# Three more output products from rounded parts, and the sums of the third right operand one step earlier

## What is computed

```python
Q = (img_embed @ Wq).reshape(B, -1, H, D).transpose(0, 2, 1, 3)
K = (sent_embed @ Wk).reshape(B, -1, H, D).transpose(0, 2, 1, 3)
V = (sent_embed @ Wv).reshape(B, -1, H, D).transpose(0, 2, 1, 3)
score = jnp.einsum('bhqd,bhkd->bhqk', Q, K) / math.sqrt(D)
attn = jax.nn.softmax(score, axis=-1)
ctx = jnp.einsum('bhqk,bhkd->bqhd', attn, V).reshape(B, -1, H * D)
out = ctx @ Wo + img_embed
return (out - mu) * jax.lax.rsqrt(var + EPS) * gamma + beta
```

## Time and profile before

| | us |
|---|---|
| median of 3 runs | 355.93 (355.36 to 355.99) |
| the profiled execution | 354.91 |
| its span, first to last instruction | 353.1 |
| granted TensorE clock, mean | 0.999 of full speed |
| PE, PEld busy | 347.5, 323.9 |
| DVE, ACT, POOL busy | 265.1, 228.6, 193.0 |

### The profile page before, as it was taken

How to read it: one execution, slowest core, us unless ns; L and a number is a source line. 1 busy time by engine, 2 the same in 40 slices (tenths; PEclk the granted TensorE clock), 3 DMA queues, 4 the chain that set the end, 5 groups by cost and what they waited for, 6 DMA issues and landing times. The chain is left out here.

```text
span 353.1 us, 6783 instructions
## 1 busy us (share of the span) xinstructions
PE 347.5 (98%) x2272; PEld 323.9 (92%) x2272; DVE 265.1 (75%) x495; ACT 228.6 (65%) x778; POOL 193.0 (55%) x208
## 2 busy tenths in 40 slices
PE   9999999999999999999999999999999999999994
PEld 6999999999999999998899899988988998899884
DVE  2159998673921277898798988987988989879896
ACT  3267764244333569887876976878768769778560
POOL 0045640000003857679679688687696796885243
PEclk9999999999999999999999999999999999999999
DMA  8999779775735070052242341541522413403003
GB/s 236 425 420 337 255 240 338 274 250 211 228 137 202 0 278 22 3 179 97 84 151 70 137 152 38 172 137 43 180 90 91 149 65 144 148 32 120 32 35 114
DMA packets 19682, 55.80 MB, mean 158 GB/s; under 512 B 1728, under 2 KB 3264, under 8 KB 17728
## 3 DMA queue, kind: packets, MB, share of 16 engines
q1 hardware_dynamic: 18784, 54.38, 42.8%
q10 hardware_dynamic: 864, 1.00, 1.1%
HBM read 46.98 MB, written 8.39 MB: 157 GB/s over the span
## 5 line engine op out<-in xcount | busy, mean ns | idle before, releaser
L646 PE MATMUL pair<-vw_hi,pt_hi 128*128 128x512 f32 x155 | 62.2, 402 | 0.0
L646 PE MATMUL pair<-vw_hi,pt_lo 128*128 128x512 f32 x155 | 60.9, 393 | 0.0
L646 PE MATMUL pair<-vw_lo,pt_hi 128*128 128x512 f32 x155 | 60.5, 391 | 0.0
L1250 POOL TENSOR_TENSOR out_sb<-centred,beta_sb 128x512 f32<-128x512 f32 x30 | 38.8, 1294 | 28.9 <-ACT centred L840 28.8
L1270 POOL TENSOR_TENSOR x_sum<-xt_in 128x256 f32<-128x256 f32 x16 | 11.9, 745 | 62.2 <-DMA xt_in<-x_tiles 62.1
L795 ACT ACTIVATE prob<-c,neg_max 128x77 f32<-128x77 f32 x128 | 44.0, 346 | 0.0
L1295 POOL TENSOR_TENSOR xo_lo<-x_sum,xo_hi 128x512 fp32r<-128x512 f32 x32 | 41.6, 1304 | 0.5 <-ACT xo_hi L819 0.5
L571 PE MATMUL pair<-a_hi,xo_hi 128*128 128x308 f32 x128 | 40.4, 316 | 0.0
L571 PE MATMUL pair<-a_hi,xo_lo 128*128 128x308 f32 x128 | 38.9, 304 | 0.0
L571 PE MATMUL pair<-a_lo,xo_hi 128*128 128x308 f32 x128 | 38.9, 304 | 0.0
L833 ACT ACTIVATE pt_hi<-pair 128x640 fp32r<-128x640 f32 x32 | 22.5, 703 | 23.5 <-PE pair L633 23.5
(11 more groups left out here) (119 smaller groups left out, 945.0 us busy)
## 6 DMA issues: line engine op xcount, KB each, us to landing
w_out<-wo SPq DMA_DIRECT2D x8, 1024.0 KB, 4.8
xt_in<-x_tiles SPq DMA_DIRECT2D x16, 512.0 KB, 3.8
x_in<-x_rows SPq DMA_DIRECT2D x16, 512.0 KB, 4.8
out<-out_sb SPq DMA_DIRECT2D x31, 256.0 KB, 2.2
w_out<-wq_t SPq DMA_DIRECT2D x7, 1024.0 KB, 7.8
w_proj<-wv SPq DMA_DIRECT2D x8, 768.0 KB, 4.7
w_proj<-wk SPq DMA_DIRECT2D x6, 768.0 KB, 9.6
w_out<-wq_t SPq DMA_DIRECT2D x2, 512.0 KB, 7.9
```

The lines of the kernel that those rows point to most:

```text
L646: mm = pe.matmul(ps_out[:, i % 2, 0:s.model], ps[:, j, :], v[:, b, j, :], start=(j == 0 and n == 0), stop=(j == s.key_t - 1 and n == len(p ...
L1250: pool.tensor_tensor(out_sb[i % OUT_RING][:, :], centred[i % 2][:, :], beta_sb[:, :], ALU.add)\
```

## The change

The output products of steps 12, 13 and 14 (`SPLIT_VALUES`, value heads 4 to 6) take the form of rounded parts. For each of these: V is rounded and split into `kv_t`; Wo is rounded by ScalarE one step ahead, behind `split_vw`, and split by VectorE; ScalarE copies the first column range into `vw_t`, and VectorE adds the second in a new step `add_out_product`, with a semaphore `dve_vw_sum` on which later transposes and products wait. A gap in memory puts `v_t1` under `kv_t1`.

Since the rests and the rounded weights use the scratch of the sums, T3 comes earlier: at step 10 VectorE splits T2 and sums T3 ahead of `split_vw`, and ScalarE rounds T3 at step 10, in the same place as T4, ahead of VW's half 0; it was at step 11. T4 and T3 are split on VectorE behind `split_vw` at step 10.

```diff
+    SPLIT_VALUES = range(H + 4, USES - 1)
...
         def whole_out(u):
 
-            return u < FULL_OUT or u >= H
+            return u < FULL_OUT or (u >= H and u not in SPLIT_VALUES)
...
             def wait_out(u, half):
 
                 if u < H:
                     pe.wait_ge(dve_a_lo, 2 * u + half + 1)
+                elif whole_out(u):
+                    pe.wait_ge(act_vw_t, 2 * (u - H) + half + 1)
                 else:
-                    pe.wait_ge(act_vw_t, 2 * (u - H) + half + 1)
+                    pe.wait_ge(dve_vw_sum, summed_before(u) + half + 1)
...
             def transpose_vw(h):
                 for j, b in plan[h]:
                     n, rows = group_no[j, b], s.key_rows(j)
                     pe.wait_ge(act_vw_t, 2 * h)
+                    pe.wait_ge(dve_vw_sum, summed_before(H + h))
...
                 if u == H + 1:
                     for part in T_PARTS[:4]:
                         round_t(*part)
-                elif u in (H + 2, H + 3):
-                    for part in T_PARTS[2 * (u - H):2 * (u - H) + 2]:
+                elif u == H + 2:
+                    for part in T_PARTS[4:]:
                         round_t(*part)
...
                     split_vw(u - H)
-                if FULL_OUT <= u + 1 < H:
+                if u + 1 < USES and not whole_out(u + 1):
                     round_w_out(u + 1)
                 take_out_product(u, 1)
...
+            def add_out_product(u, half):
+
+                cols = head_cols(vw_t, half, u - H)
+                dve.wait_ge(act_vw_t, 2 * (u - H) + half + 1)
+                dve.tensor_tensor(cols, by_batch(second(ps_outp[half])), cols, ALU.add).then_inc(dve_vw_sum, 1)
...
+                if u == H + 2:
+                    for n, task in ((T2, split_t), (T3, right_sum)):
                         for b in range(s.batches):
-                            right_sum(n, b)
-                elif u in (H + 1, H + 2):
-                    for n in ((T1, T4), (T2, T3))[u - H - 1]:
-                        for b in range(s.batches):
-                            split_t(n, b) if n in (T1, T2) else right_sum(n, b)
-                elif u == H + 3:
-                    for n in (T4, T3):
-                        for b in range(s.batches):
-                            split_t(n, b)
+                            task(n, b)
+                if not whole_out(u):
+                    add_out_product(u, 0)
+                if u == USES - 1:
+                    bias_rows()
+                split_vw(u - H)
+                if u + 1 < USES and not whole_out(u + 1):
+                    split_w_out(u + 1)
+                if not whole_out(u):
+                    add_out_product(u, 1)
+                for n, task in {H: ((T1, right_sum), (T2, right_sum)), H + 1: ((T1, split_t), (T4, right_sum)),
+                                H + 2: ((T4, split_t), (T3, split_t))}.get(u, ()):
+                    for b in range(s.batches):
+                        task(n, b)
```

More of the change, by code:

```diff
@@ L147, in build @@
         with ExitStack() as values:
-            v_t = [values.enter_context(nc.sbuf_tensor(f"v_t{n}", [P, s.dim_t, s.toks], F32)) for n in range(2)]
+            v_t0 = values.enter_context(nc.sbuf_tensor("v_t0", [P, s.dim_t, s.toks], F32))
+            values.enter_context(nc.sbuf_tensor("gap6", [P, s.dim_t, s.toks], F32))
+            v_t = [v_t0, values.enter_context(nc.sbuf_tensor("v_t1", [P, s.dim_t, s.toks], F32))]
         kv_t = [sb(f"kv_t{n}", [P, s.dim_t, 2 * s.toks], F32R) for n in range(2)]
@@ L249, in build @@
         dve_comb, dve_half_max = sem("dve_comb"), sem("dve_half_max")
+        dve_vw_sum = sem("dve_vw_sum")
         dve_centred, dve_pad, dve_last = sem("dve_centred"), sem("dve_pad"), sem("dve_last")
@@ L309, in whole_out, with split_before, summed_before @@
         def whole_out(u):
-            return u < FULL_OUT or u >= H
+            return u < FULL_OUT or (u >= H and u not in SPLIT_VALUES)
+        def split_before(u):
+            return sum(not whole_out(v) for v in range(u))
+        def summed_before(u):
+            return 2 * sum(not whole_out(v) for v in range(H, u))
         def value_of(u):
@@ L478, in wait_kv @@
                 else:
-                    pe.wait_ge(dve_kv_lo, 2 * (u - FULL_OUT) + half + 1)
+                    pe.wait_ge(dve_kv_lo, 2 * split_before(u) + half + 1)
             def project_full(u):
@@ L541, in out_product @@
                     if m % 2 == 0:
-                        pe.wait_ge(act_o_hi, 2 * (u - FULL_OUT) + half + 1)
-                        pe.wait_ge(dve_o_lo, 2 * (u - FULL_OUT) + half + 1)
+                        pe.wait_ge(act_o_hi, 2 * split_before(u) + half + 1)
+                        pe.wait_ge(dve_o_lo, 2 * split_before(u) + half + 1)
                         wait_out(u - 1, half)
@@ L548, in out_product @@
                         mm.then_inc(pe_outp, 1)
+                    if m == 2 and u >= H:
+                        transpose_vw(u - H)
             def transpose_vw(h):
@@ L936, in split_w_out @@
                 for half in range(2):
-                    dve.wait_ge(act_o_hi, 2 * (u - FULL_OUT) + half + 1)
+                    dve.wait_ge(act_o_hi, 2 * split_before(u) + half + 1)
                     dve.tensor_tensor(half_cols(w_out_lo[u % W_RING], half), half_cols(w_out_sb[u % W_RING], half),
@@ L1154, in _ @@
                     take_out_product(u, 0)
-                    if FULL_OUT <= u + 1 < H:
+                    if not whole_out(u + 1):
                         split_w_out(u + 1)
                     take_out_product(u, 1)
[L1158 to L1163, removed]
-                        for b in range(s.batches):
-                            right_sum(n, b)
-                elif u in (H + 1, H + 2):
-                    for n in ((T1, T4), (T2, T3))[u - H - 1]:
-                        for b in range(s.batches):
-                            split_t(n, b) if n in (T1, T2) else right_sum(n, b)
-                elif u == H + 3:
-                    for n in (T4, T3):
-                        for b in range(s.batches):
-                            split_t(n, b)
+                    continue
+                if u == H + 2:
+                    for n, task in ((T2, split_t), (T3, right_sum)):
+                        for b in range(s.batches):
+                            task(n, b)
[4 more added lines that the diff above has]
+                split_vw(u - H)
+                if u + 1 < USES and not whole_out(u + 1):
+                    split_w_out(u + 1)
[5 more added lines that the diff above has]
+                        task(n, b)
             add_u2(0)
```

## The result

| | before | changed |
|---|---|---|
| median of 9 runs, us | 355.74 (355.36 to 355.99) | 356.84 (356.09 to 357.27) |
| the profiled execution, us | 354.91 | 356.09 |
| its span, us | 353.1 | 354.1 |
| PE, PEld busy, us | 347.5, 323.9 | 347.2, 323.6 |
| DVE, ACT, POOL busy, us | 265.1, 228.6, 193.0 | 278.1, 233.6, 193.8 |

The changed kernel is slower: its time is 1.0035 of that of before, 95% interval 1.0026 to 1.0043, or 0.9 to 1.5 us. The forecast was 357.0, 1.11 us over a median of before of 355.93; with more runs that median is 355.74.

The account below looks back on a forecast made before the run. TensorE, running a gapless row of matmuls, was taken to bound the kernel. A 1.54 us stall less a 0.43 us gain gave + 1.11 us, 355.93 to 357.0 us; the forecast's own range was 356.5 to 357.5, 8-in-10 range 355.5 to 357.9.

Parts of the forecast that it names:

- What bounds: Weight phase: TensorE, PE busy 98% of the span, runs matmuls without gaps; work removed or stalls added count by their length.
- Part 3, the stall: Projection of step 12: TensorE waits for VW's rest, done at 90.80, wanted at 89.43; stall 1.54 us.
- the restart: After VW's rest is released in step 12's projection: TensorE's stream runs as if restarted 0.17 us later.
- Part 1, the gain: Output products of rounded parts at steps 12 to 14: 0.43 us back, bounds 0.2 and 0.45.
- the charge of 0.02 us: Steps 12 and 13: together lose 0.02 us because transposes between products of rounded parts cost 0.88 us, not 0.87.
- Part 2, no new waits: Steps 12 to 14: ScalarE's roundings and VectorE's splits and additions end in time; slack 1.1 us, or 0.5 by upper ends.
- the lower end that was kept: VectorE's splits of Wo: 1.2 us each, from 2.35 us a pair with GpSimd idle; the upper end was 1.7 each.
- The sum: Whole run: + 1.54 - 0.43 = + 1.11 us, giving a median of 357.0 us, 0.31% slower.
- No stall: Rival for step 12: ScalarE isn't held for T3, VW's rest is in time, gain alone, 355.5 us; 8%.
- New stalls at steps 12 to 14: Rival: besides the stall, VectorE's splits of Wo or additions come late, 0.8 to 1.2 us in all, 358.0 us; 12%.
- absorption in the long phase: Rival: TensorE's slack in the long phase absorbs the stall, about 355.7 us; 5%.
- columns alone: Rival for the output products of steps 12 to 14: columns count, three products save 3.15 us, 354.3 us; 2%.

Follow-up runs that it names:

- The experiment with fewer columns: Changed kernel, but rounded weights multiply 154 columns instead of 308 in the output products of steps 12 to 14, omitting part of the computation: 355.36 us, one run.
- the version with the order alone: Changed kernel without value heads of rounded parts, ScalarE's T3 roundings behind VW's half 1, T3's sums still early on VectorE: 355.30 us, ratio 0.9999.
- that kernel: Changed kernel with VectorE's order of before at step 10, ScalarE's T3 roundings behind VW's half 1, products of rounded parts kept: 359.87 us, one run.

## Why the prediction was right, point by point

- **What bounds.** TensorE without a gap, so that what is taken out or put in counts by its length: the shift at the first product, 1.10 us against the start of step 12's projection, is found again in the device's time (0.9 to 1.5 us). The long phase gave nothing back: the spans differ by 1.0 us where the first product starts 0.89 us later.
- **Part 3, the stall.** Predicted 1.54 us, measured 1.60. Its steps, in the changed trace, taking off the 0.21 us by which that execution ran ahead: T3's second rounding at 87.95, measured 87.75; VW's half 0 at 88.57, measured 88.38; the rounding of the transposes at 88.88, measured 88.68; VW's rest done at 90.80, measured 90.59; all within 0.02 us of the working. The missing 0.06 us is the restart, for which one row of the long phase gave the prediction 0.17 us. Here the next product starts at 92.39; twelve distances of 0.131 us before that is 90.82, 0.23 us behind the release at 90.59.
- **Part 1, the gain.** Predicted 0.43 us, measured 0.50. The two steps with transposes gained 0.18 and 0.16 us where 0.14 was put, so the transposes between products of rounded parts cost no more than between full ones; the charge of 0.02 us was too much. The experiment with fewer columns shows the larger part of what the columns alone leave out: at a pace of 0.11 us the sixteen matmuls of 154 columns take 0.7 us more than their columns at 2.4 GHz (an estimate, 16 x (0.110 - 0.064)). The rule of the Trainium skill, "TensorE: Matmul & The Clock Gate", section "Back-to-back issue gap", read by columns alone, would have had 1.04 us for each product (an estimate from the page), where the traces have 0.16 to 0.18. The same section of the Trainium skill says that the weight loads in a stream count as well; the loads that start 0.11 us apart agree with it.
- **Part 2, no new waits.** None came. The splits of Wo took 2.36 us a pair for the products of steps 12 and 13, the lower end that was kept, and 2.90 for that of step 14, beside GpSimd's sums, between the two ends. The seed of bank A was held by `bias_rows` for 0.37 us and reached the long phase in time.
- **The sum.** That 1.11 stands so near 1.10 is luck in its last digits: the stall was put 0.06 us too low and the gain 0.07 too low, the two cancel, and the device's time gives the difference only to 0.3 us either way.
- **The rivals.** No stall: shown to be what the change would have been with ScalarE's roundings elsewhere (355.2 us), not what it was. New stalls at steps 12 to 14, absorption in the long phase, columns alone: excluded by the rows above.
- **Left open.** Whether the 0.5 us of the products, plain in every trace, are worth 0.5 us on the device's clock or less: 0.32, give or take 0.33, was measured.

The version with the roundings behind VW's half 1 has the lowest time of those run: 0.9991 and 0.9990 of before in two sets of runs, 0.13 and 0.28 us under the medians of before in their sets, where the changed kernel is 1.10 us over in its own. It isn't clear of the version with the order alone.

## What to carry to other kernels

When a step is moved earlier on one engine, its consumer on another engine moves in a list too: ask what is queued behind that consumer, and whether the producer ends in time for its new place. Here one engine's idle time was filled well, and the next engine stood in front of the only thing that the bottleneck wanted; the repair was to move two instructions by a few places. Where something other than their columns spaces the matmuls, as here at 154 columns, fewer columns save less than they promise: count what neighbouring products of the same form take in the trace.

## What the runs showed of the hardware that was not expected

A wait of TensorE of 1.6 us left the granted clock at 1.00; one of 3.06 us was followed by about 0.7 us at 1.00 and then some 3.4 us at 0.50 (worked out from the means of 0.67, 0.50 and 0.96 in the stretches), and cost 1.75 us beyond its own length. The shorter wait was seen in three traces, the longer in one. The estimate for that kernel had only the wait in it.

The stall and the stretches behind it in the changed kernel, for comparison with the 0.67 and 0.50 above:

```profile
89.22:90.74 1.52, 0.17 (x3) 0.03 (x1) 1.44 (x3) 1.17 (x4) 0.00 (x0) 1.00 0.64 269
90.74:92.39 1.65, 1.65 (x13) 1.65 (x14) 1.65 (x3) 0.00 (x0) 0.00 (x0) 1.00 0.73 308
92.39:96.59 4.20, 4.20 (x35) 4.20 (x34) 2.31 (x5) 2.34 (x4) 0.00 (x0) 1.00 0.60 191
```
